# Softmax key sums in groups of three tiles, with the third tile added by a DMA from GpSimd

## The reference, cut to what matters

```python
x = x + attention(layernorm(x))       # x: (16, 1024, 256) float32
x = x + gated_layer(layernorm(x))     # gates, a scan over 16 batches, tanh

# attention: 16 score heads of width 16, in 8 pairs
scores = einsum('bhtd,bhsd->bhts', q, k)      # q, k after rotation and scaling
probs  = softmax(scores, axis=-1)
diff   = probs[:, :, 0] - lam * probs[:, :, 1]
attn   = einsum('bhts,bhsd->bhtd', diff, v)
attn   = attn * rsqrt(mean(attn * attn) + 1e-5) * (1 - LAMBDA_INIT)
```

## Time and profile before

| | before |
|---|---|
| median of 3 runs | 5260.5 us (5259.5 to 5261.4) |
| profiled execution, its own time | 5259.7 us |
| span of that execution | 5257.9 us |
| mean granted PE clock | 0.979 of full speed |
| PE busy | 4979.5 us |
| DVE busy | 4021.4 us |
| POOL busy | 2891.7 us |
| ACT busy | 2722.8 us |

### The profile page before, as it was taken

One profiled execution on the slowest core, in us unless ns is written; L12 is line 12 of the kernel. 1 busy time (PEld: TensorE's weight loads), 2 busy tenths in 40 slices (PEclk: granted clock), 3 DMA queues, 4 the chain that ended last, 5 costly groups with the idle time before them and its releaser, 6 DMA issues.

```text
span 5257.9 us, 65030 instructions
## 1 busy us (share of the span) xinstructions
PE 4979.5 (95%) x24784; PEld 1695.8 (32%) x24784; DVE 4021.4 (76%) x6183; ACT 2722.8 (52%) x3173; POOL 2891.7 (55%) x2118
## 2 busy tenths in 40 slices
PE   6999999999999999999999999999999999999999
PEld 2224232332423223242332423233242322323237
DVE  6877777877778877777887777787777887777526
ACT  1464645556465554545556454554546555463652
POOL 3573746647275573727657374664727557372750
PEclk7899999999999999999999999999999999999999
DMA  6031221302222131222303122130222213122117
GB/s 141 26 60 46 50 64 37 69 37 58 52 45 69 33 64 40 45 66 51 67 26 62 45 45 69 34 72 37 54 56 45 69 33 61 43 45 59 65 49 280
DMA packets 127706, 311.05 MB, mean 59 GB/s; under 512 B 27297, under 2 KB 30498, under 8 KB 113442
## 3 DMA queue, kind: packets, MB, share of 16 engines
q1 hardware_dynamic: 124178, 289.33, 23.2%
q10 hardware_dynamic: 3216, 17.57, 0.9%
HBM read 172.07 MB, written 99.61 MB: 52 GB/s over the span
## 4 chain that ended last, share of the span: by engine, by line
PE 64%; DVE 16%; issue 13%; POOL 3%; ACT 3%; DMA 0%; ACTq 0%; POOLq 0%; SPq 0%; DVEq 0%
PE o_ps L792 15%; PE s_ps L749 15%; PE st L777 13%; PE sum_ps L807 8%; DVE neg_max L1043 7%; PE st L891 3%; PE st L735 3%; POOL pair_sum L472 2%; PE st L717 2%; PE st L957 2%; ACT probs L564 2%; DVE stats L983 2%; DVE xa L1026 1%; DVE swapped L1021 1%; PE st L870 1%
## 5 line engine op out<-in xcount | busy, mean ns | idle before, releaser
L472 POOL TENSOR_TENSOR pair_sum<-probs 128x512 f32<-128x512 f32 x2048 | 2795.4, 1398 | 1436.4 <-ACT probs L564 1432.2
L1043 DVE TENSOR_REDUCE neg_max<-s_ps 128x1 f32<-128x512 f32 x4096 | 2679.4, 687 | 817.4 <-PE s_ps L749 810.1
L564 ACT ACTIVATE probs<-st 128x1024 f32<-128x1024 f32 x2048 | 1983.6, 1022 | 1240.9 <-PE st L777 996.0
L749 PE MATMUL s_ps<-k_stack,q_stack 96*128 96x512 bf16 x4096 | 1525.8, 393 | 140.9 <-DVE neg_max L1043 122.7
L777 PE MATMUL st<-q_stack,k_stack 99*128 99x512 bf16 x4096 | 1226.9, 385 | 20.2 <-ACT xa L512 6.6
L792 PE MATMUL o_ps<-probs,values 128*32 128x512 f32 x8192 | 1103.6, 611 | 0.7 <-ACT probs L564 0.7
L749 PEld LDWEIGHTS s_ps<-k_stack,q_stack 96*128 96x128 bf16 x4096 | 371.1, 97 | 1524.3 <-DVE neg_max L1043 1260.6
L777 PEld LDWEIGHTS st<-q_stack,k_stack 99*128 99x128 bf16 x4096 | 348.3, 99 | 792.6 <-ACT probs L564 414.8
L807 PE MATMUL sum_ps<-pair_sum,ones 128*32 128x512 f32 x4096 | 543.4, 602 | 7.7 <-POOL pair_sum L472 5.7
L891 PE MATMUL st<-xt,weights 128*128 128x512 f32 x768 | 381.7, 594 | 11.8 <-ACT xt L521 11.8
L891 PE MATMUL st<-cell_t,weights 128*128 128x512 f32 x768 | 362.9, 592 | 0.0
(11 more groups left out here) (129 smaller groups left out, 2980.3 us busy)
## 6 DMA issues: line engine op xcount, KB each, us to landing
q_stack<-qk_parts SPq DMA_DIRECT2D x384, 128.0 KB, 4.3
k_stack<-qk_parts SPq DMA_DIRECT2D x378, 128.0 KB, 7.0
swapped<-xa SPq DMA_DIRECT2D x128, 256.0 KB, 2.4
qk_parts<-swapped SPq DMA_DIRECT2D x64, 512.0 KB, 2.8
xa<-in_x SPq DMA_DIRECT2D x16, 1024.0 KB, 6.1
qk_parts<-low_part SPq DMA_DIRECT2D x64, 256.0 KB, 3.0
probs<-in_x SPq DMA_DIRECT2D x16, 1024.0 KB, 10.2
x_rows<-probs SPq DMA_DIRECT2D x16, 1024.0 KB, 3.9
```

The lines of the kernel that those rows point to most:

```text
L472: pool.tensor_tensor(pair_sum[q % 2][:, h, :], probs[a % 4][:, h, :], probs[(a + 1) % 4][:, h, :], ALU.add)\
L564: act.activation(probs[kk % 4][:, 2 * hp:2 * hp + 2, :], st[hp][:, :, :], ACT.Exp).then_inc(exp_done, 1)
L749: pe.matmul(s_ps[i % 2][:, :], q_stack[g][0:SROWS, s, t * P:(t + 1) * P], k_stack[g][0:SROWS, s, h * HALF:(h + 1) * HALF], start=True, sto ...
L1043: dve.tensor_reduce(neg_max2[:, at, i % 2:i % 2 + 1], s_ps[i % 2][:, :], AX.X, ALU.max, negate=True).then_inc(max_done, 1)
```

## The change

POOL now adds two tiles as before, and for the first two of three groups in a round a DMA, issued by POOL, adds a third tile to the buffer in SBUF. A round's eight tiles are therefore three groups, of 3, 3 and 2, and there are 12 key sums in a unit where there were 16. The key sums stand at steps 8r+6, 8r+10 and 8r+11, directly behind the weighted product of that step. Sums 10 and 11 of a unit both stand after the work between units. DVE's work after a round stands one step later. ACT's wait for a free `probs` buffer goes by the new DMA (`third_in`) for tiles 2 and 5 of a round.

```diff
+GROUPS = 3
+SUMS_AT = {8 * r + at: GROUPS * r + p for r in range(ROUNDS) for p, at in enumerate((6, 10, 11))}
-WORK = [[(ROPE_WORK if s in at else 0) + (4 if s > 8 and s % 8 == 3 else 0)
+WORK = [[(ROPE_WORK if s in at else 0) + (4 if s > 8 and s % 8 == 4 else 0)
-    room = [SUM_STEP if s % 2 == 0 and s >= 4 else 1 for s in range(STEPS)]
+    room = [SUM_STEP if s in SUMS_AT else 1 for s in range(STEPS)]
...
-                sp.wait_ge(sum_done, 32 * b + 31)
+                sp.wait_ge(sum_done, 24 * b + 23)
                 sp.dma_start(x2, x[b, :, :]).then_inc(xr_in, 16)
...
             def pair(u, g, q):
-                pool.wait_ge(exp_done, 64 * u + 4 * q + 4)
+                r, p = divmod(q, GROUPS)
+                a = KT * r + 3 * p
+                pool.wait_ge(exp_done, 64 * u + 2 * (a + 2))
                 if u > 0 or q > 1:
-                    pool.wait_ge(sum_done, 16 * u + q - 1)
-                a = 2 * q
+                    pool.wait_ge(sum_done, 12 * u + q - 1)
                 for h in range(4):
                     pool.tensor_tensor(pair_sum[q % 2][:, h, :], probs[a % 4][:, h, :],
                                        probs[(a + 1) % 4][:, h, :], ALU.add)\
                         .then_inc(pair_added, 1)
+                if p < 2:
+                    pool.wait_ge(pair_added, 48 * u + 4 * (q + 1))
+                    pool.wait_ge(exp_done, 64 * u + 2 * (a + 3))
+                    pool.dma_start(flat(pair_sum[q % 2][:, :, :]),
+                                   flat(probs[(a + 2) % 4][:, :, :]), accum_op=ALU.add)\
+                        .then_inc(third_in[p], 16)
...
                         act.wait_ge(av_done, 32 * u + (kk - 3))
-                        act.wait_ge(pair_added, 64 * u + 4 * (kk // 2 - 1))
+                        was, r, kt = (u, *divmod(kk - 4, KT)) if kk >= 4 else (u - 1, 3, kk + 4)
+                        if kt in (2, 5):
+                            act.wait_ge(third_in[kt // 3], 16 * (4 * was + r + 1))
+                        else:
+                            act.wait_ge(pair_added, 48 * was + 4 * (GROUPS * r + kt // 3 + 1))
...
                 act.wait_ge(at_ready, 4 * b + 3)
-                act.wait_ge(sum_done, 32 * b + 31)
+                act.wait_ge(sum_done, 24 * b + 23)
                 for i in range(3):
                     act.activation(square[:, i, :], part(i), ACT.Square).then_inc(sq_ready, 1)
...
             def key_sums(u, g, q):
-                r, p = q // 4, q % 4
-                pe.wait_ge(pair_added, 64 * u + 4 * (q + 1))
+                r, p = divmod(q, GROUPS)
+                if p < 2:
+                    pe.wait_ge(third_in[p], 16 * (4 * u + r + 1))
+                else:
+                    pe.wait_ge(pair_added, 48 * u + 4 * (q + 1))
...
                     if s >= 1:
                         weighted(u, g, s - 1)
-                    for i in todo[2:4]:
-                        score(un, 1 - g, i)
-                    if s >= 4 and s % 2 == 0:
-                        key_sums(u, g, (s - 4) // 2)
-                    for i in todo[4:]:
+                    if s in SUMS_AT:
+                        key_sums(u, g, SUMS_AT[s])
+                    for i in todo[2:]:
                         score(un, 1 - g, i)
                 weighted(u, g, STEPS - 1)
-                key_sums(u, g, 14)
...
                 turn_max(u + 1)
                 if not last:
                     qk(1, b, ab)
-                key_sums(u, 0, 15)
+                key_sums(u, 0, 10)
+                key_sums(u, 0, 11)
...
                     rows_out(VAL, W_V, xt, b, ab, js=(0, 1),
                              beside=(u + 2, 0, itertools.islice(late, LATE[0])))
-                key_sums(u + 1, 1, 15)
+                key_sums(u + 1, 1, 10)
+                key_sums(u + 1, 1, 11)
...
-                    if s > 8 and s % 8 == 3:
+                    if s > 8 and s % 8 == 4:
                         r = s // 8 - 1
                         turn_sums(u, g, r)
...
-                    if s > 8 and s % 8 == 4:
+                    if s > 8 and s % 8 == 5:
                         combine(u, g, s // 8 - 1)
```

More of the change, by code:

```diff
@@ L213, in build @@
         sum_done = sem("sum_done")
+        third_in = [sem("third_in0"), sem("third_in1")]
         o_read = sem("o_read")
@@ L491, in iteration @@
                 for g in range(G):
-                    for q in range(4 * ROUNDS):
+                    for q in range(GROUPS * ROUNDS):
                         pair(2 * b + g, g, q)
@@ L807, in key_sums @@
                     mm = pe.matmul(sum_ps[32 * h:32 * h + 32, :], ones[:, 0:32],
-                                   pair_sum[q % 2][:, h, :], start=(p == 0), stop=(p == 3))
+                                   pair_sum[q % 2][:, h, :], start=(p == 0), stop=(p == GROUPS - 1))
                 mm.then_inc(sum_done, 1)
@@ L1068, in turn_sums @@
                 sum_turned = attn_t[:, g, r // 2 * HALF:(r // 2 + 1) * HALF]
-                dve.wait_ge(sum_done, 16 * u + 4 * (r + 1))
+                dve.wait_ge(sum_done, 12 * u + 3 * (r + 1))
                 dve.transpose(sum_turned, sum_ps[:, :]).then_inc(sum_step, 1)
```

## The result

The changed kernel takes 5465.5 us (median of 4 runs, 5456.9 to 5471.2) against 5260.0 us beside it: a ratio of 1.039, interval 1.037 to 1.041. I had forecast 5200 us, with 5085 to 5350 as the range, so the forecast was wrong in sign and the time lies outside the range. The profiled execution took 5456.9 us. The period of the batch read here is 324.9 us, where it was 311.7 (L489 recurs at 2705.53 and 3030.46 us).

What follows compares the result with a forecast made beforehand. PE was taken to bound a unit's second half, PE, DVE and POOL nearly together the first. 5259.7 - 152 (PE) - 15 (POOL, DVE) + 19 (between units) + 87 (DMA) = 5199, said as 5200 us; range 5085 to 5350.

Steps and rivals of the forecast that it cites:

- the DMA's term: Loss from PE waiting for the new accumulating DMA: 87 us, from 0 to 365 us.
- Directly behind a weighted product the set costs 0.86 us: PE's price for key sums adjoining a weighted product, against 1.10 us for a set that stands apart.
- rival C: DVE takes over, PE waits for maxima (sign: `neg_max` waits well above 123 us); 5256 us, chance 0.08.
- What leaves PE: Key sums on PE shrink from 541 to 338 us, so PE's own work falls by 203 us.
- How much reaches the end: Share of PE's 203 us that shortens the kernel: 75%, 152 us, between 50% and all.
- The DMA's length: Issue to landing beside the wait-free 6.4 us: 40 rounds at 6.6 and 56 at 8.0 lose 8 + 84.
- the loop: Sums, freed buffer, POOL adds, DMA, next sums: PE waits if the DMA exceeds 6.4 us; 96 rounds exposed.
- the other groups have slack: DMAs outside the loop cost nothing; the second group's has until step 8r+10, over 9 us.
- Between units: At a batch's end squares and copies on ACT delay PE's mean squares: 1.2 us per batch, 19 us.
- POOL and DVE: 512 fewer POOL adds ease DVE's rotations: at most 78 us of DVE, 15 us of end time.
- One DMA's landing: Issue to landing of the 1 MB accumulating DMA: about 6.5 us when quiet, 3.9 to 10.2.
- Rival D: Slower: the DMA loop decides; gain gone at mean landing 7.9 us, 5352 us at 8.9; chance 0.28.

Runs made afterwards that it cites:

- small_dma: Changed kernel with the accumulating DMA cut to 128x128 of one head, order, waits and semaphores kept: 5309.6 us, ratio 1.009 to the kernel before.
- small_9_between: Changed kernel with second group's sums at step 8r+9, two scores between weighted product and sums, and the DMA cut to 128x128: 5195.3 us, ratio 0.9874.
- pos_9_between: Changed kernel with second group's sums at step 8r+9 and two scores between weighted product and key sums, full-size DMA: 5238.5 us, ratio 0.9956.
- two_between: Changed kernel with two scores put back between the weighted product and the key sums, nothing else: 5432.4 us, ratio 1.032.
- before_skip: Kernel before, with the second of each round's four key sums reduced to one 32x32 product: 5223.4 us, ratio 0.9928.
- groups_2_3_3: Changed kernel with groups of 2, 3, 3 tiles, sums at 8r+6, 8r+8, 8r+11, two scores between, squares waiting for adds: 5590.2 us, ratio 1.062.

## Why the prediction was wrong

Without the DMA's term the sum of the prediction was 5260 - 152 - 15 + 19 = 5112; `small_dma`, with that term cut to almost nothing, took 5310. So 198 of the 266 us that are missing lie in the terms for PE's work and its place, and 69 in the DMA's (156 us where I had 87).

The 205 us between the kernel before and the changed one can also be walked step by step, each between two measured kernels: fewer sets of sums with two scores between and a short DMA, -66 (5261 to `small_9_between`); the DMA at full size, +43 (`pos_9_between`); the second sums at step 10, +194 (`two_between`); sums directly behind, +33 (the changed kernel). What a step is worth depends on the order: placement alone is worth 149 us in the kernel before, 140 with sums at step 9, 75 with a short DMA at step 10, and 33 where it hides behind the waits for the DMA.

- **"Directly behind a weighted product the set costs 0.86 us"** is the step that failed first. The price is right for PE alone and was read at a unit's end, where no score follows. In the steps that matter, the scores that used to stand between feed DVE; without them the third score waits for a maximum, and the set costs 1.60 instead of 1.10 us. Moving the sets in the kernel before cost 149 us, where these prices promise a gain. I had seen the five scores packed into a step and put it in rival C at 8%; C's sign, PE's wait for `neg_max` well above 123 us, came (250).
- **What leaves PE**: I said that the key sums would be busy about 340 us, and they are 406. A set takes 1.06 us of busy time before (543.4 / 512) and after (405.7 / 384); the busy column doesn't tell where a set stands, and that 541 agreed with 543 was luck. So the 203 us are a sum of chain prices that no run shows: 141 of them are the 128 sets that are gone, the rest is the new place, which cost time.
- **How much reaches the end** was wrong too: I took 75%. The runs show 27% of at most 141 us (`before_skip`) and about half of 129 (`small_9_between`). The latter also has a quarter fewer adds on POOL; what of its gain is due to them wasn't measured by itself. I had taken a stretch in which PE is busy as one in which all of PE's gain arrives; in `before_skip` the waits for POOL and for maxima grew by 56 and 47 us instead.
- **The DMA's length** cost 156 us where I had 87 (8 + 84 is 92; there was no reason to round it down). The landing in the loop was sized about right: the first groups of rounds 2 to 4 landed after 7.2 us on average, and my 40 rounds at 6.6 and 56 at 8.0 are 7.4. What failed is "the other groups have slack". The time from one step's key tile to the next, summed over all units, is 145 us longer in the trace of the changed kernel than in that of `small_dma`, and the steps tell where. The steps 8r+6 and 8r+7 of rounds 2 to 4, where the loop's tile is due, are 37 us longer and those of the first round 30. The steps 8r+1 and 8r+2, where ACT needs the buffer of the second group's third tile, are 88 us longer, and all others 10 shorter. So the loop cost less than my 87 us and the second group's DMA, priced at nothing, the most. In the third round of a unit it landed after 9.4 us in the median, and up to 11.9.
- **Between units** I took 19 us. PE's mean squares follow the sums without a gap, as before (they start at 3007.84 and take 2.84 us, like those at 2908.99), although ACT now waits 91 us for these sums in all. In the batch read here nothing is lost there beyond the moved set; no run measures the term by itself.
- **POOL and DVE**: the rotation line's median fell from 2236 to 1222 ns, further than I had said, and DVE's busy time by 95 us. No gain from it can be seen in the time: DVE waited 1061 us for scores. The adds on POOL, which I expected nearer 1.3 than 1.4 us, have a mean of 1.42, where it was 1.40.
- **One DMA's landing**: by the Trainium skill's fit (page "DMA: Bandwidth & Descriptors", section "Anatomy of one DMA — SWDGE (gpsimd) path"), 4.4 us for a plain copy and 6.8 with a second read was the estimate. The measured 7.0 agrees with the second.
- **Rival D** (slower, through the loop) had the right side and half of the mechanism. It asked for a mean landing of 8.9 us to reach 5352; with the placement's cost beside it, a median of 7.0 (mean 7.6) was enough.

## What to carry to other kernels

A busy engine at 95% is not a promise that work taken from it comes back: look who is second, or take a little work away and measure the share that arrives. Before instructions are put side by side for the sake of one engine, ask what the ones in between were feeding; with two buffers between them, the third of a burst waited for the first one's reader. For a slow transfer, list every reader and every next writer of both its tiles and take the earliest of them, not the one that you have in mind; here the next exp came before the sums. The place where a buffer is freed was worth as much (194 us) as the transfer's length (198).

## What the runs showed of the hardware

An accumulating DMA of 1 MB inside SBUF, issued by POOL, occupies POOL for 0.88 us and lands after 7.0 us at the least and in the median, 4.6 for half the size and 2.4 for 64 KB: 2.4 us for the second half megabyte. Others are slowed beside it: the median of the loads of `q_stack` went from 4.3 to 6.9 us (4.3 again in `small_dma`). Beside SP's loads it took 11.6 and 13.2 us in the rows above, and 13.8 at the most in the changed kernel.

In the changed kernel PE's clock fell after PE had stood idle. The windows of the changed kernel around the wait above (PE, PEld, DVE, ACT, POOL busy, PE clock, DMA share, GB/s):

```profile
2962.00:2968.00 6.00, 5.43 (x35) 1.23 (x35) 4.05 (x7) 3.84 (x4) 2.23 (x3) 1.00 1.07 316
...
2976.00:2980.00 4.00, 3.65 (x14) 1.02 (x18) 1.38 (x2) 3.25 (x4) 0.00 (x0) 0.58 1.10 159
```

After 2.40 us of idleness the granted clock was 0.58 over the next 4 us, most of it at the lower of the two levels (1.2 instead of 2.4 GHz), and a weighted product took 1.59 us in the chain instead of 0.99. The mean granted clock was 0.979 before, 0.971 in the changed kernel, 0.967 in `two_between` and 0.953 in `groups_2_3_3`: a wait for a DMA can cost more than its own length. The prediction has no term for this. It can be some 48 us of PE's full-speed time at the most, an estimate from the clocks and spans: 0.029 x 5455 - 0.021 x 5258. How much of the 205 us it is was not measured by itself.
